# Mixer chain: the three unread products in front of each step's C-times-B product are removed

## The reference, cut to what matters

```
def step(carry, inp):
    z, xs = carry
    Bt, Ct, At, dtt, St, ut = inp
    d = dtt[..., None, None]
    a = At[..., None, None]
    s = St[..., None, None]
    bu = Bt[..., :, None] * ut[..., None, :]
    z = s * (z - d * a * xs + d * bu)
    xs = xs + d * z
    y = jnp.einsum('bhn,bhnp->bhp', Ct, xs)
    return ((z, xs), y)
```

## Time and profile before

| What | us |
|---|---|
| median of three runs | 1820.72 |
| lowest and highest | 1814.13 and 1826.43 |
| the profiled execution's own time | 1814.29 |
| its span, first to last instruction | 1812.5 |
| TensorE busy | 1481.0 |
| VectorE busy | 1311.4 |
| ScalarE busy | 1052.1 |
| GpSimd busy | 383.6 |

### The profile page before, as it was taken

One profiled execution on the slowest core, in us unless ns is written; L12 is line 12 of the kernel. 1 busy time (PEld: TensorE's weight loads), 2 busy tenths in 40 slices (PEclk: granted clock), 3 DMA queues, 4 the chain that ended last, 5 costly groups with the idle time before them and its releaser, 6 DMA issues. The chain is left out here.

```text
span 1812.5 us, 36735 instructions
## 1 busy us (share of the span) xinstructions
PE 1481.0 (82%) x14334; PEld 1115.6 (62%) x14334; DVE 1311.4 (72%) x2831; ACT 1052.1 (58%) x1872; POOL 383.6 (21%) x393
## 2 busy tenths in 40 slices
PE   5898996886359879899999755997297899999795
PEld 5888985785235567674444545997286544446474
DVE  5988895589839755648997556886556369994666
ACT  6998895432258726455898323664101548995555
POOL 0000000000436510127960104674000320000100
PEclk9999998687659999897999757999598879999898
DMA  5120001000000010004530182121200000000101
GB/s 141 27 64 22 19 2 35 14 1 4 1 7 2 2 33 1 14 2 137 179 107 2 45 250 57 60 63 45 70 1 14 1 1 2 2 2 1 34 1 36
DMA packets 52725, 67.97 MB, mean 38 GB/s; under 512 B 11511, under 2 KB 41465, under 8 KB 52554
## 3 DMA queue, kind: packets, MB, share of 16 engines
q1 hardware_dynamic: 46586, 50.74, 9.2%
q0 software_dynamic: 3840, 9.18, 1.7%
q10 hardware_dynamic: 2128, 5.71, 1.3%
HBM read 46.97 MB, written 18.65 MB: 36 GB/s over the span
## 5 line engine op out<-in xcount | busy, mean ns | idle before, releaser
L2022 DVE TENSOR_REDUCE att_max<-banks 104x1 f32<-104x512 f32 (+1 forms) x480 | 295.9, 682 | 9.2 <-PE banks L1936 5.0
L2057 ACT ACTIVATE att_p<-banks 104x514 f32<-104x514 f32 (+1 forms) x480 | 262.0, 599 | 33.4 <-PE banks L1981 22.5
L339 PE MATMUL banks<-tok_wT,feature_halves 128*128 128x192 f16 x2592 | 229.7, 249 | 22.8 <-DVE feature_halves L365 11.7
L339 PEld LDWEIGHTS banks<-tok_wT,feature_halves 128*128 128x128 f16 x2592 | 217.4, 99 | 32.0 <-DVE feature_halves L365 17.4
L1997 PE MATMUL banks<-att_p,att_v 104*32 104x257 f32 (+1 forms) x1920 | 159.6, 405 | 0.9 <-ACT att_p L2057 0.3
L1981 PE MATMUL banks<-att_q,att_kT 64*104 64x257 f16 (+1 forms) x960 | 156.0, 304 | 2.9 <-ACT att_p L2057 2.5
L1936 PE MATMUL banks<-att_kT,att_q 64*104 64x512 f16 (+1 forms) x480 | 126.4, 424 | 4.6 <-DVE att_max L2022 2.1
L134 PE MATMUL banks<-ones 128*128 128x256 f16 x594 | 82.1, 296 | 56.7 <-PEq L113 26.6
L365 DVE TENSOR_TENSOR feature_halves<-features,feature_halves 128x2048 f16<-128x2048 f32 x54 | 123.3, 2283 | 6.2 <-ACT feature_halves L462 6.2
L1981 PEld LDWEIGHTS banks<-att_q,att_kT 64*104 64x104 f16 (+1 forms) x960 | 61.9, 123 | 106.7 <-ACT att_p L2057 79.4
L462 ACT CAST feature_halves<-features 128x2048 f16<-128x2048 f32 x54 | 102.2, 1893 | 11.0 <-PE banks L339 10.2
(11 more groups left out here) (464 smaller groups left out, 3421.2 us busy)
## 6 DMA issues: line engine op xcount, KB each, us to landing
expert_w_in<-in_L_ffn_w_dram SPq DMA_DIRECT2D x16, 576.0 KB, 4.6
expert_w_halves<-expert_w_halves SPq DMA_DIRECT2D x32, 288.0 KB, 2.3
tok_w<-in_L_tok_W_dram ACTq DMA_DIRECT2D x4, 1152.0 KB, 7.4
expert_w2s<-expert_w_halves SPq DMA_DIRECT2D x1, 4608.0 KB
expert_y<-expert_out SPq DMA_DIRECT2D x6, 513.0 KB
expert_w1s<-expert_w_halves SPq DMA_DIRECT2D x2, 1536.0 KB
raw<-in_x_dram SPq DMA_DIRECT2D x2, 1152.0 KB, 5.7
expert_w1s<-expert_w_halves SPq DMA_DIRECT2D x3, 768.0 KB
```

The lines of the kernel that those rows point to most:

```text
L339: ins = pe.matmul(c.bank[t // 2][:, (t % 2) * D:(t % 2 + 1) * D], fh[:, s, q, z, t * 128:(t + 1) * 128], wT[:, y, k, 6 * q + wf, :], start ...
L2022: dve.reduce_max(mx[0:qn, n // NS % 2, 2 * gi + e, k:k + 1], bank_of(unit)[0:qn, 0:KEYS], X).then_inc(maxed, 1)
L2057: act.activation(p[0:kn, n % 4, :, :], c.pair[2 + n % 2][0:kn, :].rearrange("p (e q) -> p e q", e=2)[:, :, 0:HALF], ACT.Exp, scale=scale). ...
```

## The change

The call of `spin` inside `c_times_b` is taken out, and with it 108 products and 108 weight loads. The 36 products ahead of the first `c_times_b` stay, and so does every wait. A blank line above goes as well, so lines in the new kernel are one or two lower than before. No other engine's list changes.

```diff
@@ -1338,7 +1337,6 @@
                 if n >= 2:
                     pe.wait_ge(wt_ready, n - 1)
                 ps = c.bank[2 + n % 2][0:L, 0:SH * L]
-                spin(c, pe, 3, 2 + n % 2)
                 pe.matmul(ps, half.b[:, cols], cbd[:, n % 2, :, :].rearrange("p a b -> p (a b)"),
                           start=True, stop=False)
                 pe.matmul(ps, half.bl[:, cols], cbd[:, n % 2, :, :].rearrange("p a b -> p (a b)"),
```

## The result

The changed kernel took **1838.48 us** (median of seven runs, 1832.98 to 1848.47) against 1819.57 us for the kernel before, timed beside it (seven runs, 1814.13 to 1826.43). The ratio is **1.0109, 95% interval 1.0079 to 1.0138**: slower by 1.1%, or 19.8 us. That is inside the range of the forecast, 15.8 us above its point, and it is rival C that came true: the clock was lost in the first steps and did not come back before the last steps of the chain. One run of a later kernel, the one with six unread products in each group, took 2211.86 us at a mean clock of 0.629 and is in no ratio here; all other runs of all kernels are.

What follows compares the result with a forecast made beforehand. It took a VectorE-ScalarE ring of 2.55 us a step as the chain's bound. Start -0.3 and low-clock steps +2.3 gave +2.0 us: 1816.3 us on the profiled execution, 1822.7 us on the median, range 1814 to 1845 us.

Steps and rivals of the forecast that it cites:

- rival C: Chain: clock falls in the first steps and stays at 0.50 to its end; +20 us, 1840.7 us; chance 0.28.
- The ring and its cover: Chain steps: VectorE and ScalarE in turn set 2.55 us, hiding TensorE's 0.43 us of unread products; removal gains nothing.
- The start: Group ahead of the first product: VectorE waits for TensorE there, so fewer unread products give -0.3 us.
- The fall in the first steps: Chain's first six steps: TensorE has least work at 541 to 544.4 us, so a clock fall is likelier than not.
- The row at 402 us: Elsewhere in the trace: 1.79 us of TensorE work in a like stretch was followed by a clock fall.
- The price of a low step: Chain step at the low clock: 3.2 us against 2.55, +0.65 us each; first four steps cost nothing.
- Does it come back?: Chain from the fifth step: TensorE's full work restores the clock after three or four low steps; +2.3 us.
- at 1317 us: Elsewhere in the trace: 3.40 us of full TensorE work on transposes at 0.50 was followed by clock 1.00.
- the 14 us with 13.76 us busy: Elsewhere in the trace: nearly full TensorE work on other small products stayed at clock 0.50 throughout.
- A: Chain: clock falls early and comes back; +1 to +5 us; the forecast itself, chance 0.45.
- Rival B: Chain: the clock never falls, only -0.3 us at its beginning remains, 1820.4 us; chance 0.22.
- D: Mixing matrix's low half: TensorE finishing earlier moves GpSimd's operand away from it; up to -9 us, 1812 us; chance 0.05.

Runs made afterwards that it cites:

- the burst: Changed kernel plus 24 unread products at once in the ninth C-times-B group, none in other steps: ratio 1.0000 against the kernel before, chain 104.5 us.
- the rise at 543 us: Clock's return in the kernel before with unread products removed from the first eight C-times-B groups only: ratio 1.0038, chain 101.1 us.

## Why the prediction was right, and where it was not

**The ring and its cover: right.** Where neither TensorE's list is fuller nor GpSimd's operand is moved, the step at 1.00 is 2.52 to 2.56 us, with three, one or no unread products, and the wait for the low half of u grew to 0.56 us (0.6 forecast).

**The start: right.** -0.4 us, against -0.3.

**The fall in the first steps: right**, at 541 to 542 us, in the window that I had pointed to. In the four kernels that had the 36 products in front and none in the early steps it happened, and with one a step it came later. The row at 402 us that I set beside it was weak support: TensorE did nothing there for the 1.4 us before the fall.

**The price of a low step: right in kind.** 3.31 us against 3.2, so +0.77 us and not +0.65. The first steps cost nothing, as said.

**"Does it come back?": wrong, and this is the step that failed.** I took a return after three or four low steps, +2.3 us, and gave it 0.45. The runs showed none in 27 long steps, 26 of them at about +0.77 us, which are the 20 us; that was the case to which I had given 0.28. The term rested on full work bringing the clock back, as at 1317 us. The changed kernel's TensorE is busy 93.00 us of 93.00 from 549 us on, and the clock stayed at 0.50 all the same, as in the 14 us with 13.76 us busy, which was the nearer row. Part of this busy time is not needed: the same products took 3.15 us in another order, 0.16 us less. Why the clock stayed is not shown. A step of 3.15 us was followed by a return in the one profile taken of it, steps of 3.31 us never were in two kernels, and one product more a step was enough.

**C's size: right, in part by luck.** +20 us forecast, +20.8 us in the chain. My sum had given 28 x 0.65 = 18.2 us, and I rounded it up for spread; the low step was 0.12 us dearer than I had put. The measured time lies in the stated range only because I had stretched it into C; the point was A's.

Rival B is refuted by the trace. D's mechanism, the 0.82 us low half, is real, but TensorE's earlier finish does not move it: it still takes 0.82 us in the kernel with unread products in the first eight groups only. At the low clock it fell to 0.50 us, where VectorE had time to spare. It took a wait on GpSimd and another order on TensorE to win most of it.

The Trainium skill's rule on transposes ("TensorE: Matmul & The Clock Gate", Part 4: PE-mode transpose), by which C would have been the forecast, is not made right by C: the steps after the burst hold the clock, but no run here takes the transposes out, so none tells whether they count in the chain.

Left open: why the clock came back in some low stretches and not in others, with the same instructions once (the rise at 543 us above). The profiles are one or two to a kernel; that the changed kernel behaves so in all its runs is supported by the mean clock of its seven, 0.848 to 0.860, against 0.872 to 0.891 in the 83 runs of the kernel before that were timed with the experiments.

## What to carry to other kernels

Work that keeps a clock up has to be judged at the thinnest place of a loop, not at its mean: here the first four steps decide, and the unread products of the last 28 groups could go without a cost. When a loop can lose the clock, work out its step at the low clock too; if TensorE is then the bound, the loop can stay there for its whole length. One burst at the entry of the full steps is an insurance: here it cost the chain 4.3 us against the kernel before and saved 16.4 against the changed one. A busy share of 100% in a record of small products is no proof that the engine has nothing to gain: the same products took 3.31 or 3.15 us, with 100% in both.

## What the runs showed of the hardware that was not expected

- The loop has two lasting states with the same instructions: 2.54 us a step at 1.00 (after a burst, 24 intervals between mixing matrices without a fall) and 3.31 us at 0.50 (26 without a rise).
- One unread product a step (256 columns) instead of three is enough to leave the low state, after about 10 us.
- Work that fills TensorE's record does not always bring the clock back: 93.00 us busy of 93.00 at 0.50 in the changed kernel. In the first steps the same instructions once gave a rise some 3 us after the fall, and in two other profiles none.
- At the low clock the same products took 3.31 us a step in one order and 3.15 us, in the one step recorded, in another.
- VectorE's subtraction of 57 x 342 numbers into 16 bits takes 0.50 us alone and 0.82 us with GpSimd's product of 112 x 342 beside it; GpSimd's takes 0.76 us either way.
